# A Mamba block with its RWKV feed-forward on one core: the mix of r moved into scaled weights, the norms' small scalars moved to ScalarE, and new tables of turns

## The chip, the cores and the metric

The kernel runs on one core of a Trainium2 chip. The metric is the time on the device in microseconds (us), as the median of several runs. The core's engines work side by side, each through its own list of instructions in order, and they meet only through semaphores: TensorE (PE in the profile) multiplies matrices out of SBUF into PSUM, VectorE (DVE) and ScalarE (ACT) work elementwise on SBUF and PSUM, GpSimd (POOL) works elementwise on SBUF, and SyncE (SP) issues the transfers.

## The reference

Everything is float32: x has 4 sequences of 2048 tokens with 256 channels, the state has N = 16 columns for each channel.

```python
x = x + mamba(layernorm(x))
x = x + ffn(layernorm(x))

def mamba(x_in):
    x, z = split(x_in @ W_in)
    proj = x @ W_x                       # raw delta, B (16), C (16)
    delta = softplus(proj[..., :D] @ W_dt + b_dt)
    h_t = exp(delta_t * A) * h_{t-1} + (delta_t * x_t) * B_t      # for each of 16 columns
    y_t = sum over the columns of h_t * C_t,   y = y + x * D_param
    res = (y * silu(z)) @ W_out + x_in
    return layernorm(res) * ln_g + ln_b

def ffn(h):                              # h_prev: h of the token before, 0 at the start
    hr = mu_r * h + (1 - mu_r) * h_prev
    hk = mu_k * h + (1 - mu_k) * h_prev
    r = sigmoid(hr @ W_r.T);  k = hk @ W_k.T
    return r * (square(relu(k)) @ W_v.T)
```

## The kernel before

The 8192 tokens are cut into 16 chunks of 512 (`NT`), four to a sequence. A chunk has channels on the partitions (two halves of 128, index m, h or k) for the scan, and tokens on the partitions (four blocks of 128, `TB`) for the norms. The kernel is software-pipelined over steps t = -1 to 17. In step t the scan of chunk t runs, the part ahead of it (norm 1, the projections, softplus) is done for chunk t+1 (`pre`), the gate, the output projection and the norms 2 and 3 for chunk t-1 (`mid`), and the feed-forward for chunk t-2 (`end`). Step -1 is the head with tables of its own, steps 16 and 17 are the tail.

Each step has 16 turns, one for each state column n. In turn n:

- GpSimd makes `dbx` of column n+3 (`times_b`, 128x1024), and for the columns outside `SPLIT` the product of column n-1 with C (`times_c`). These are 16 + 9 products in a step.
- ScalarE makes the two exponentials of column n+1 into PSUM (`exps`). For three banks `da_ps` the exponential of a half must wait until VectorE is done with the half three places back. ScalarE also keeps the carries, and has all that turns, norms, activates and evacuates.
- VectorE scans column n in two halves, and does the product with C itself for the 7 columns of `SPLIT`. It also has the softplus differences, u, the gate, the affine part of norm 2, the feed-forward's mixes and its output product.
- TensorE adds the transposed product of column n - `Y_LAG` into `y_ps` (`add_up`, 8 matmuls), and does all projections and transposes in three banks `w0_ps` to `w2_ps`.

Where in a step's 16 turns each other unit stands is written out by hand, in tables: `ACT_TURN`, `VEC_TURN`, `PE_TURN` and `POOL_TURN` for the full steps, with `..._HEAD` and `..._TAIL` for both ends. `BANK` says in which of the three banks a unit's result is put. A unit waits for the unit ahead of it in its bank to be read. Since every engine goes through its list in order, a unit that has to wait holds up everything behind it, the exponentials, scans or products of the next columns among it.

What the change touches: `hT_in` on ScalarE (L596, L597) copies the transposed h out of PSUM twice, shifted by a token, once scaled by 1 - mu_k (`xk`) and once by 1 - mu_r (`xr`). `mix` on VectorE (L859) adds mu_k h and mu_r h to them, in two instructions for each half. `by_token` on TensorE (L966) multiplies `xr` with `w_rT`. The tanh of r (L681) reads the result. The norms: ScalarE sums and squares with accumulators, `rsqrt` makes `rs` (L522, L524), GpSimd makes `nm` of norm 3 (L483) and the products `nr` = `nm` x `rs` of norms 1 and 3 (`scale_mean`, L442), and ScalarE's `norm` (L501) reads them. On SyncE nothing of this stands.

## Time and profile before

| | before |
|---|---|
| median of 3 runs | 1037.73 us (1037.49 to 1039.17) |
| the profiled execution | 1038.93 us, its span 1037.2 us |
| busy: PE, DVE, ACT, POOL | 905.7, 925.7, 907.3, 939.1 us |
| mean granted TensorE clock | 0.934 of full speed |
| first and last start of GpSimd's `nm` in a step with a scan | 143.47 and 977.29 us |

The span is what the trace covers, and the profiled execution took 1.7 us more than it. All four engines are busy for 87 to 91% of the span. The share of a step is better read from a stretch of whole steps: from 203.1 to 859.1 us there are 11 of them, 59.64 us each. In the timeline each row gives start, duration, engine, line, operation and the tiles out<-in, and in brackets how long the engine was idle ahead of it and who ended that. A row of several instructions spans them all. Neighbours on one engine overlap in these rows by about 0.1 us.

### The profile page before, as it was taken

What the parts mean: (1) busy time and instruction counts of PE and PEld (TensorE: products, weight loads), DVE (VectorE), ACT (ScalarE), POOL (GpSimd) and SP (SyncE); (2) the same over time, 40 slices, a digit from 0 to 9 for tenths busy, and PEclk for the clock granted to TensorE, in tenths of its full rate; (3) what the DMA queues carried; (4) which work ended last, traced back from release to release, by engine and by line L of the source; (5) the groups of instructions that cost most, each with busy time, mean ns of one, the idle gap of its engine ahead of it and who ended that gap; (6) DMA issues with size and microseconds to landing.
All of it is one profiled execution on the core that took longest, in us unless ns stands there. A gap on an engine that the chain in (4) does not pass through costs nothing. (4 is left out here: it accounts for less than half of the span.)

```text
span 1037.2 us, 15069 instructions
## 1 busy us (share of the span) xinstructions
PE 905.7 (87%) x4728; PEld 699.3 (67%) x4728; DVE 925.7 (89%) x1003; ACT 907.3 (87%) x2041; POOL 939.1 (91%) x455
## 2 busy tenths in 40 slices
PE   6485888989898998989899898989989898996976
PEld 3254576867767686776768577676858677684954
DVE  0799899999999999999999999999999999999933
ACT  5886889999989999999989999999999999886753
POOL 0799999999999999999999999999999999999810
PEclk9797898999899998999999998999989998998998
DMA  4534454444535544463455545354554445254111
GB/s 141 218 123 185 166 203 182 163 166 179 189 135 212 187 184 158 170 223 125 183 186 183 195 150 206 129 203 161 187 219 151 178 166 207 100 206 180 62 41 41
DMA packets 51039, 172.21 MB, mean 166 GB/s; under 512 B 5392, under 2 KB 31760, under 8 KB 34576
## 3 DMA queue, kind: packets, MB, share of 16 engines
q1 hardware_dynamic: 50960, 171.25, 45.0%
q8 instruction: 38, 0.62, 0.2%
q14 instruction: 41, 0.34, 0.1%
HBM read 153.41 MB, written 9.44 MB: 157 GB/s over the span
## 5 line engine op out<-in xcount | busy, mean ns | idle before, releaser
L450 POOL TENSOR_TENSOR dbx<-u,b_ring 128x1024 f32<-128x1024 f32 x256 | 602.5, 2371 | 0.7 <-DVE u L850 0.7
L545 ACT ACTIVATE da_ps<-delta,a_neg 128x512 f32<-128x512 f32 x512 | 334.7, 682 | 38.8 <-DVE hg L802 14.1
L463 POOL TENSOR_TENSOR hg<-hg,c_ring 128x1024 f32<-128x1024 f32 x144 | 341.9, 2374 | 3.8 <-DVE hg L802 3.8
L952 PEld LDWEIGHTS y_ps<-ident,hg 128*128 128x128 f32 x2048 | 252.0, 149 | 74.0 <-issue 48.3
L952 PE MATMUL y_ps<-ident,hg 128*128 128x128 f32 x2048 | 277.1, 286 | 15.4 <-POOL hg L463 14.6
L802 DVE TENSOR_TENSOR_SCAN hg<-da_ps,carry,dbx 128x512 f32<-128x512 f32 x216 | 264.1, 1267 | 12.8 <-ACT da_ps L545 12.5
L802 DVE TENSOR_TENSOR_SCAN da_ps<-da_ps,carry,dbx 128x512 f32<-128x512 f32 x168 | 206.1, 1272 | 1.1 <-ACT da_ps L545 1.1
L809 DVE TENSOR_TENSOR hg<-da_ps,c_ring 128x1024 f32<-128x1024 f32 x112 | 137.2, 1225 | 12.0 <-DVE da_ps L802 0.5
L802 DVE TENSOR_TENSOR_SCAN hg<-da_ps,dbx 128x512 f32<-128x512 f32 x72 | 84.5, 1207 | 7.9 <-ACT da_ps L545 7.6
L972 PE MATMUL w_ps<-ident,h_tok 128*128 128x128 f32 x128 | 26.9, 350 | 60.9 <-DVE mixed L859 60.8
L959 PE MATMUL w_ps<-mixed,w_kT 128*128 128x512 f32 x128 | 64.9, 632 | 6.8 <-DVE mixed L859 3.7
L966 PE MATMUL w_ps<-w_rT,mixed 128*128 128x256 f32 x256 | 65.9, 413 | 3.2 <-DVEq L833 1.6
L802 DVE TENSOR_TENSOR_SCAN da_ps<-da_ps,dbx 128x512 f32<-128x512 f32 x56 | 65.3, 1210 | 0.1
L966 PEld LDWEIGHTS w_ps<-w_rT,mixed 128*128 128x128 f32 x256 | 52.8, 212 | 15.8 <-DVE mixed L859 3.4
L972 PEld LDWEIGHTS w_ps<-ident,h_tok 128*128 128x128 f32 x128 | 18.8, 176 | 64.7 <-DVE mixed L859 64.3
L959 PE MATMUL w_ps<-xnT,w_in 128*128 128x512 f32 x120 | 60.0, 624 | 1.6 <-ACT xnT L560 1.6
L966 PE MATMUL w_ps<-w_out,gated 128*128 128x256 f32 x256 | 60.5, 379 | 0.0
L966 PE MATMUL w_ps<-w_in,xnT 128*128 128x256 f32 x240 | 57.4, 382 | 3.0 <-ACT delta L588 3.0
L966 PE MATMUL w_ps<-w_vT,kact 128*128 128x256 f32 x256 | 58.3, 380 | 1.9 <-ACT kact L687 1.0
L959 PE MATMUL w_ps<-xT,w_dtx 128*128 128x512 f32 x124 | 58.5, 594 | 0.4 <-ACT bc_rows L657 0.4
L966 PEld LDWEIGHTS w_ps<-w_in,xnT 128*128 128x128 f32 x240 | 46.1, 193 | 17.3 <-issue 8.2
L966 PEld LDWEIGHTS w_ps<-w_vT,kact 128*128 128x128 f32 x256 | 47.3, 190 | 8.8 <-issue 1.9
(134 smaller groups left out, 1468.5 us busy)
## 6 DMA issues: line engine op xcount, KB each, us to landing
b_ring<-bc_rows_dram SPq DMA_DIRECT2D x64, 1024.0 KB, 5.3
c_ring<-bc_rows_dram SPq DMA_DIRECT2D x64, 1024.0 KB, 4.7
x_tok<-in_L_attn_x_in_dram SPq DMA_DIRECT2D x16, 512.0 KB, 5.8
res<-xn_tok SPq DMA_DIRECT2D x16, 512.0 KB, 3.2
xres<-in_L_attn_x_in_dram SPq DMA_DIRECT2D x16, 512.0 KB, 4.7
out_dram<-r_out SPq DMA_DIRECT2D x15, 512.0 KB, 3.0
bc_rows_dram<-bc_rows SPq DMA_DIRECT2D x16, 64.0 KB, 1.6
w_in<-in_L_attn_W_in_dram SPq DMA_DIRECT2D x1, 512.0 KB, 4.8
```

What stands on the lines that cost most here:

```text
L450: pool.tensor_tensor(dbx[:, n % X_RING, :, :], u[:, ip, :, :], b.to_broadcast([P, KH, LC]), ALU.mult).then_inc(s["dbx_done"], 1)
L463: pool.tensor_tensor(part, part, c_of(n).to_broadcast([P, KH, LC]), ALU.mult).then_inc(s["g_pool"], 1)
L545: act.activation(da_of(n, h), delta[:, ip, h, :], ACT.Exp, scale=a_neg[:, h, n:n + 1]).then_inc(s["da_ready"], 1)
L802: dve.tensor_tensor_scan(out, da_of(n, h), dbx[:, n % X_RING, h, :], 0.0 if first else carry[:, n, h:h + 1], ALU.mult, ALU.add).then_inc(s ...
L809: dve.tensor_tensor(hg[:, n % H_RING, :, :], da_both(n), c_of(n).to_broadcast([P, KH, LC]), ALU.mult).then_inc(s["g_vec"], 1)
L952: last = pe.matmul(y_tok[:, b, h * P:(h + 1) * P], hg[:, n % H_RING, h, b * P:(b + 1) * P], ident[:, :], is_transpose=True, start=n == 0 a ...
L959: last = pe.matmul(out, w[:, k, cols], x[:, k, :], start=k == 0, stop=k == KH - 1)
L966: last = pe.matmul(by_block(out)[:, b, :], xT_[:, k, tokens], w[:, k, :], start=b == 0 and k == 0 and not begun, stop=k == KH - 1, skip_gr ...
L972: last = pe.transpose(bank[:, j * P:(j + 1) * P], src[:, j, k * P:(k + 1) * P], ident[:, :])
```

## The change

It has four parts.

1. **r.** xr @ W_r.T is written as h @ (mu_r W_r.T) + h_prev @ ((1 - mu_r) W_r.T). ScalarE makes the two scaled copies `w_rT` and `w_r_prev` once in the head, in four instructions in place of one. In a step, `hT_in` copies h unscaled into `h_of`, VectorE's `mix` has one instruction for each half in place of two, and TensorE's `r_by_token` has 16 matmuls of 256 columns (each two instructions in the trace) in place of 8.
2. **Small scalars.** ScalarE makes `nr` of norms 1 and 3 behind `rs`, in four copies of 128x1 with a scale from a column each, and `nm` of norm 3 in one copy of 128x4. The squares of norm 3 take `nm` as bias, like those of norm 1. GpSimd has none of the three any more.
3. **Tables.** All turns and banks are new, and `Y_LAG` is 2 in place of 1.
4. The statistics of W_out are put into the carry's buffer, and `POOL_TURN` and `POOL_HEAD` are gone.

```diff
-B_LEAD, C_LAG, Y_LAG = 3, 1, 1
+B_LEAD, C_LAG, Y_LAG = 3, 1, 2
...
-POOL_TURN = dict(nm3=11, nr3=13, nr1=15)
...
+VEC_TURN = dict(mix0=3, mix1=3, gate=5, sp0=5, u0=6, sp1=9, u1=10, x20=10, x21=10, v0=12, v1=12)
...
-            def scale_mean(ln, count):
-                need(pool, ln_rs[ln], count)
-                pool.tensor_tensor(nr[ln][:, :], nm[ln][:, :], rs[ln][:, :], ALU.mult).then_inc(ln_nr[ln], 1)
...
-                    if mid and n == turn["nm3"]:
-                        need(pool, *((ln_sum_end, 2) if at_end(t) else (ln_sum[3], t)))
-                        pool.tensor_tensor(nm[3][:, :], sum3[:, :], minus_1_d[:, :], ALU.mult).then_inc(s["nm3_done"], 1)
-                    if more and n == turn["nr1"]:
-                        scale_mean(1, t + 3)
-                    if mid and n == turn["nr3"]:
-                        need(pool, s["nm3_done"], t)
-                        scale_mean(3, t)
...
+                if ln in nr:
+                    need(act, ln_rs[ln], count)
+                    for j in range(TB):
+                        last = act.activation(nr[ln][:, j:j + 1], nm[ln][:, j:j + 1], ACT.Copy, scale=rs[ln][:, j:j + 1])
+                    last.then_inc(ln_nr[ln], 1)
...
-                    act.activation(xr[:, m, 1:LC + 1], b[:, :], ACT.Copy,
-                                   scale=omr[:, m:m + 1]).then_inc(mixed_prev[m], 1)
+                    act.activation(h_of[:, m, 1:LC + 1], b[:, :], ACT.Copy).then_inc(mixed_prev[m], 1)
...
+                            if m == 0:
+                                act.wait_ge(s["omu_set"], 2)
+                                for k in range(KH):
+                                    act.activation(w_r_prev[:, k, :], turned[:, k, :], ACT.Copy, scale=omr[:, k:k + 1])
+                                    last = act.activation(w_rT[:, k, :], turned[:, k, :], ACT.Copy, scale=mur[:, k:k + 1])
...
+                        act.activation(nm[3][:, :], sum3[:, :], ACT.Copy, scale=-1.0 / D).then_inc(ln_sum[3], 1)
                     if mid and at("sq3"):
...
+                        squares(xres[:, nxt, :, :], 3, h_tok, t)
...
-                    for x, mu in ((xk, muk), (xr, mur)):
-                        part = x[:, m, 0:LC]
-                        last = dve.scalar_tensor_tensor(part, b[:, :], mu[:, m:m + 1], part, ALU.mult, ALU.add)
-                    last.then_inc(read_sem(t, f"hT{m}"), 1)
+                    part = xk[:, m, 0:LC]
+                    dve.scalar_tensor_tensor(part, b[:, :], muk[:, m:m + 1], part, ALU.mult,
+                                             ALU.add).then_inc(read_sem(t, f"hT{m}"), 1)
...
+            def r_by_token(out, v):
+
+                for b in range(2):
+                    at_b = (2 * v + b) * P
+                    for k in range(KH):
+                        pe.matmul(by_block(out)[:, b, :], h_of[:, k, at_b + 1:at_b + 1 + P], w_rT[:, k, :], start=k == 0,
+                                  stop=False)
+                    for k in range(KH):
+                        last = pe.matmul(by_block(out)[:, b, :], h_of[:, k, at_b:at_b + P], w_r_prev[:, k, :], start=False,
+                                         stop=k == KH - 1)
+                return last
```

**GpSimd, where `nm` and `nr` stood.** From a full step before (`nm` is norm 3's negative mean, `nr` a norm's bias), and then the same columns after the change:

```order
L463 TENSOR_TENSOR hg<-hg,c_ring 128x1024
L483 TENSOR_TENSOR nm<-sum,minus_d 128x4
L450 TENSOR_TENSOR dbx<-u,b_ring 128x1024 x2
```

```order
L457 TENSOR_TENSOR hg<-hg,c_ring 128x1024
L444 TENSOR_TENSOR dbx<-u,b_ring 128x1024 x3
```

The list is now products only, and nothing in it waits for ScalarE's norms.

**ScalarE, norm 3.** Before, from the evacuation of the second residual (`xres`) to the norm's output (`h_tok`); `da_ps` are the exponentials:

```order
L728 ACTIVATE xres,sum<-w_ps 128x256 x4
L545 ACTIVATE da_ps<-delta,a_neg 128x512 x2
L588 ACTIVATE delta<-w_ps 128x512
L737 ACTIVATE h_tok,sq<-xres,sum 128x256 x4
L522 ACTIVATE lv<-sq,eps 128x4
L524 ACTIVATE rs<-lv 128x4
L545 ACTIVATE da_ps<-delta,a_neg 128x512 x2
L560 ACTIVATE zs<-w_ps 128x512
L501 ACTIVATE h_tok<-xres,nr,rs 128x256 x4
```

After the change, from the same evacuation on:

```order
L723 ACTIVATE xres,sum<-w_ps 128x256 x4
L730 ACTIVATE nm<-sum 128x4
L533 ACTIVATE da_ps<-delta,a_neg 128x512 x2
L498 ACTIVATE h_tok,sq<-xres,nm 128x256 x4
L505 ACTIVATE lv<-sq,eps 128x4
L507 ACTIVATE rs<-lv 128x4
L511 ACTIVATE nr<-nm,rs 128x1 x4
L533 ACTIVATE da_ps<-delta,a_neg 128x512 x2
```

The small scalars now stand on ScalarE's own list, ahead of the next pair of exponentials. Norm 1 has the same four copies.

**TensorE, around the feed-forward's first half.** Before, from the transposes of `h_tok` to the evacuated x (`w_kT` comes some rows later):

```order
L952 MATMUL y_ps<-ident,hg 128x128 x32
L972 MATMUL w_ps<-ident,h_tok 128x128 x8
L952 MATMUL y_ps<-ident,hg 128x128 x8
L972 MATMUL w_ps<-ident,xn_tok 128x128 x8
L966 MATMUL w_ps<-w_rT,mixed 128x256 x8
L959 MATMUL w_ps<-xnT,w_in 128x512 x2
```

After the change, from the same transposes to the softplus addition (`ln_v`):

```order
L975 MATMUL w_ps<-ident,h_tok 128x128 x8
L943 MATMUL y_ps<-ident,hg 128x128 x8
L950 MATMUL w_ps<-xT,w_dtx 128x512 x2
L950 MATMUL w_ps<-mixed,w_kT 128x512 x2
L966 MATMUL w_ps<-w_rT,mixed 128x256 x2
L969 MATMUL w_ps<-w_r_prev,mixed 128x256 x2
L1079 MATMUL w_ps<-ln_v,ident 128x512
```

The pair of `w_rT` and `w_r_prev` rows stands four times there. The transposes of `xn_tok` and the projection of x now come ahead of those of `h_tok`, and the two halves of the transposed h are in two banks (0 and 2) where they shared bank 2.

## Rows read from the trace of the kernel before

**Rows 1.** GpSimd's timeline: start, duration, line, operation, tiles, [idle before]

```profile
33.73 11.65 POOL L450 TENSOR_TENSOR dbx<-u,b_ring 128x1024 f32<-128x1024 f32 x5 [0.71 <-DVE u L850]
...
143.47 0.20 POOL L483 TENSOR_TENSOR nm<-sum,minus_d 128x4 f32<-128x4 f32 x1 [0.70 <-ACTq L732]
...
561.11 0.20 POOL L483 TENSOR_TENSOR nm<-sum,minus_d 128x4 f32<-128x4 f32 x1 [1.33 <-DVE u L850]
...
918.79 0.20 POOL L483 TENSOR_TENSOR nm<-sum,minus_d 128x4 f32<-128x4 f32 x1 [0.97 <-ACTq L732]
```

**Rows 2.** Busy time by stretch: the sum of eleven steps, 203.1 to 859.1 us

```profile
sum 656.00, PE 606.02 PEld 473.04 DVE 626.80 ACT 617.84 POOL 643.34; mean PE 55.09 PEld 43.00 DVE 56.98 ACT 56.17 POOL 58.48
```

**Rows 3.** VectorE's waits, the same stretch: in total, times, longest us

```profile
DVE hg L802 <- ACT da_ps L545: 9.3, 15, 1.3
...
DVE hg L809 <- DVE da_ps L802: 0.5, 1, 0.5
```

**Rows 4.** ScalarE's waits, the same stretch

```profile
ACT xT L560 <- PE w_ps L959: 5.5, 11, 0.6
...
ACT r_out L681 <- PE w_ps L966: 3.8, 8, 0.7
...
ACT da_ps L545 <- DVE hg L809: 0.7, 3, 0.2
```

**Rows 5.** TensorE's timeline in one full step, around its longest idle stretch

```profile
500.35 1.04 PE L952 MATMUL y_ps<-ident,hg 128*128 128x128 f32 x8
501.23 3.62 PE L966 MATMUL w_ps<-w_vT,kact 128*128 128x256 f32 x16
504.68 1.89 PE L966 MATMUL w_ps<-w_in,xnT 128*128 128x256 f32 x8
...
517.53 1.12 PE L972 MATMUL w_ps<-ident,h_tok 128*128 128x128 f32 x4 [4.13 <-DVE mixed L859]
518.44 1.92 PE L952 MATMUL y_ps<-ident,hg 128*128 128x128 f32 x8
520.15 1.91 PE L972 MATMUL w_ps<-ident,xn_tok 128*128 128x128 f32 x8
521.86 4.29 PE L966 MATMUL w_ps<-w_rT,mixed 128*128 128x256 f32 x16
```

**Rows 6.** VectorE's timeline in the same step

```profile
516.74 0.74 DVE L859 SCALAR_TENSOR_TENSOR mixed<-w_ps,mur,mixed 128x512 f32<-128x512 f32 x1
517.39 2.33 DVE L802 TENSOR_TENSOR_SCAN hg<-da_ps,dbx 128x512 f32<-128x512 f32 x2
...
528.81 1.22 DVE L802 TENSOR_TENSOR_SCAN hg<-da_ps,dbx 128x512 f32<-128x512 f32 x1 [1.18 <-ACT da_ps L545]
```

**Rows 7.** ScalarE's timeline in the same step

```profile
515.18 0.67 ACT L597 ACTIVATE mixed<-w_ps,omr 128x512 f32<-128x512 f32 x1
...
540.62 0.57 ACT L564 ACTIVATE kact<-w_ps 128x512 f32<-128x512 f32 x1
...
554.30 0.30 ACT L522 ACTIVATE lv<-sq,eps 128x4 f32<-128x4 f32 x1
554.63 0.21 ACT L524 ACTIVATE rs<-lv 128x4 f32<-128x4 f32 x1
554.74 1.28 ACT L545 ACTIVATE da_ps<-delta,a_neg 128x512 f32<-128x512 f32 x2
```

**Rows 8.** All engines' timeline at the end of the last scan and in the tail

```profile
987.66 2.35 POOL L463 TENSOR_TENSOR hg<-hg,c_ring 128x1024 f32<-128x1024 f32 x1 [3.84 <-DVE hg L802]
...
1008.67 1.06 ACT L687 ACTIVATE kact<-kact 128x1024 f32<-128x1024 f32 x1
...
1014.64 1.06 PE L972 MATMUL w_ps<-ident,h_tok 128*128 128x128 f32 x8
...
1019.45 3.78 PE L959 MATMUL w_ps<-mixed,w_kT 128*128 128x512 f32 x4 [3.74 <-DVE mixed L859]
1023.02 2.81 PE L966 MATMUL w_ps<-w_rT,mixed 128*128 128x256 f32 x8
```

**Rows 9.** ScalarE's timeline in the head

```profile
9.37 2.07 ACT L501 ACTIVATE xn_tok<-x_tok,nr,rs 128x256 f32<-128x256 f32 x4 [0.32 <-POOL nr L442]
```

More of the change, by code:

```diff
@@ new lines @@
+VEC_HEAD = dict(wdtx=3, sp0=5, sp1=9, u0=9, u1=9, center=11)
+PE_HEAD = dict(xnT0=0, xnT1=0, x0=0, x1=5, bc=6, dt0=8, dt1=9, z1=9, z0=12, la0=14, la1=14, ffn=14)
+POOL_TAIL = dict(xb=13)
+ACT_TAIL = dict(prev=0, hT1=0, hT0=1, k1=3, gT0=3, gT1=3, sq20=5, sq21=5, rs2=6, k0=9, square=9, sum30=9, sum31=12,
+                sum3_set=12, sq3=12, rs3=12, silu=15, norm3=15)
+VEC_TAIL = dict(mix1=2, mix0=3, gate=3, x20=8, x21=11, v0=12, v1=14)
+PE_TAIL = dict(hT0=0, hT1=0, k1=2, gT0=2, gT1=2, wo0=3, wo1=4, k0=8, r0=9, r1=11, v0=13, v1=14)
@@ L61 @@
+TAIL_BANK = dict(hT1=1, wo1=1, k1=0, wo0=0, gT0=1, k0=2, v0=1, gT1=2, v1=2, hT0=2, r1=0, r0=2)
 W_BANKS = 3
@@ L184, in mamba_rwkv_layer @@
         mixed = sb("mixed", P, 2, KH, LC + 1)
-        xk, xr = mixed[:, 0, :, :], mixed[:, 1, :, :]
+        xk, h_of = mixed[:, 0, :, :], mixed[:, 1, :, :]
         kact = sb("kact", P, KH, LC)
         r_out = sb("r_out", P, TB, D)
+        carry_raw = carry[:, :, :].rearrange("p n k -> p (n k)")
+        w_stats = [carry_raw[:, 6 * k:6 * k + 6] for k in range(KH)]
+        w_mean = [carry_raw[:, 12 + 2 * k:14 + 2 * k] for k in range(KH)]
         W_LOADS = 13
@@ L466, in step @@
                 nxt = 1 - par
-                turn = of_step(t, POOL_HEAD, POOL_TURN, POOL_TAIL)
-                if t == -1:
-                    scale_mean(1, 1)
                 for n in range(NS):
@@ L476, in step @@
                         times_c(behind[0], behind[2])
-                    if mid and at_end(t) and n == turn["xb"]:
+                    if mid and at_end(t) and n == POOL_TAIL["xb"]:
                         need(pool, s["xres_loaded"], 16 * t)
@@ L713, in step @@
                             turned = work[m % 2][:, :].rearrange("p (k n) -> p k n", k=KH)
-                            act.activation(w[:, :, :], turned, ACT.Copy, scale=scale).then_inc(s["ffn_ev"], 1)
+                            if m == 0:
[3 more added lines that the diff above has]
+                                    last = act.activation(w_rT[:, k, :], turned[:, k, :], ACT.Copy, scale=mur[:, k:k + 1])
+                            else:
+                                last = act.activation(w[:, :, :], turned, ACT.Copy, scale=scale)
+                            last.then_inc(s["ffn_ev"], 1)
                     if pre and at("z_set"):
@@ L729, in step @@
                             last.then_inc(ln_sum_end if at_end(t) else read_sem(t, f"wo{v}"), 1)
-                    if mid and not at_end(t) and at("sum3_set"):
-                        need_all_read(act, t, ["wo0", "wo1"])
-                        act.sem_inc(ln_sum[3], 1)
-                    if mid and at("sq3"):
-                        need(act, *((ln_sum_end, 2) if at_end(t) else (ln_sum[3], t)))
-                        for j in range(TB):
-                            last = act.activation(h_tok[:, j, :], xres[:, nxt, j, :], ACT.Square, scale=-float(D),
-                                                  bias=sum3[:, j:j + 1], accum_out=sq[3][:, j:j + 1])
-                        last.then_inc(ln_sq[3], 1)
+                    if mid and at("sum3_set"):
+                        if at_end(t):
+                            need(act, ln_sum_end, 2)
+                        else:
+                            need_all_read(act, t, ["wo0", "wo1"])
+                        act.activation(nm[3][:, :], sum3[:, :], ACT.Copy, scale=-1.0 / D).then_inc(ln_sum[3], 1)
+                    if mid and at("sq3"):
+                        squares(xres[:, nxt, :, :], 3, h_tok, t)
                     if mid and at("rs3"):
-                        rsqrt(3, t, of=float(D * D))
+                        rsqrt(3, t)
                     if mid and at("norm3"):
@@ L1029, in post_unit @@
                         else:
-                            last = by_token(out, m, xr, w_rT)
+                            last = r_by_token(out, m)
                     else:
```

49 lines of the change are left out of this document (18 added, 31 removed).

## The prediction

> **What bounds the kernel now.** I read the timeline of GpSimd first, since the page gives it the largest busy share. The reader is to see where it waits. It starts its products at 33.73 us, five of them take 11.60 us to the next start (start plus duration, less the usual overlap), so one costs 2.32 us, and 25 of them 58.0 us for a step. Its `nm` starts at 143.47 and, 13 steps later, at 918.79 [rows 1]: 775.32 / 13 = 59.64 us for a step. The missing 1.64 us are its three small products (about 0.15 each) and the wait ahead of `nm`, which was 0.70 to 1.33 in the rows shown. That wait ends on ScalarE or VectorE, never the other way round. In the stretch of eleven steps nobody but TensorE waited for GpSimd, and that for 0.3 us in all. So GpSimd is the fullest engine and still follows the others; something else sets 59.64.
>
> Next the busy time by stretch and the waits. VectorE has a mean of 56.98 us busy in 59.64 [rows 2], and four kinds of waits, of which the first and last are shown, sum to 20.1 us in eleven steps, 1.83 a step [rows 3]; its work with the gaps that it cannot avoid is then 59.64 - 1.83 = 57.8. ScalarE has nine kinds of waits with a sum of 26.8, 2.44 a step [rows 4]; its need is 57.2. TensorE waits once a step for VectorE's mix, 4.13 us in the row shown, since both halves of h use one bank, and works slowly behind it [rows 5]: the granted clock there is the lower of its two levels (1.2 GHz), as the same eight transposes into `y_ps` take 1.92 us behind the idle stretch and 1.04 ahead of it. So four lists of 57.2 to 58.5 us interlock within a column or two, and 1.2 to 2.4 us of each step is scattered waiting: first for x, r, k and the rest that the late TensorE delivers [rows 4], and then VectorE for the exponential behind the silu, 1.18 us [rows 6]. The chain runs through three engines.
>
> **The change part by part.** The sum is made for a step, for the 13 between the two `nm` above, against the profiled execution of 1038.93 us (span 1037.2), which is 1.20 above the median 1037.73.
>
> VectorE sheds two mix instructions. One goes from 516.74 to 517.39 [rows 6], so 2 x 0.65 = 1.30, and its need falls to 56.5. That alone buys little, since it is no longer the longest list.
>
> GpSimd sheds its three small products and the wait. Its need is 58.0, and nothing but the products themselves can hold it.
>
> TensorE gains 8 matmuls, 16 instructions, of 256 columns. The nearest row is `w_vT`: 16 in 501.23 to 504.68, 3.45 us at full clock, and the r of before took 4.12 (521.86 to 525.98) behind the idle stretch [rows 5]. I take 3.45. It also loses the idle 4.4 us (48.6 in eleven steps), as the halves of h are in two banks, and with it the slow work. From the starts shown that is 518.44 to 520.15 in place of 0.88, 520.15 to 521.86 likewise, 0.67 of r and 0.47 of the transposes of h, 2.8 in all [rows 5]. Its need is 59.64 - 4.4 - 2.8 = 52.4 before and 55.9 after. The extra work is therefore covered, as long as no stretch of 4 us without work comes back. If that cover is gone it costs the 3.45 again, and more at the lower clock.
>
> ScalarE gains. The copy of h without a column as scale is 0.10 shorter (0.67 against 0.57 of a copy with a constant [rows 7]), twice, so -0.19 or so. `nm` adds one small copy, 0.10. Each `nr` adds a wait for its own `rs` (0.21 long, where the next instruction came after 0.11), 0.12, and four copies. The trace has no 128x1 copy with a column as scale. It is bounded by `rs`, a constant scale: 0.21 long and 0.11 to the next start, and by `lv`, which takes a column as operand: 0.30 long, so 0.20 to the next start if the extra 0.09 occupies the engine [rows 7]. I take 0.19, nearer to `lv`, since the operand is of that kind. Two groups are 2 x (0.12 + 4 x 0.19) = 1.76, at the low end 1.12. Altogether +1.67 (low end +1.03): ScalarE's need rises from 57.2 to 58.9 (58.2), which makes it the longest list.
>
> A rule of the Trainium skill speaks against the change here. ScalarE: Activation LUTs, in What ACT_TABLE_LOAD costs, says that an activation with a column operand is about 93 ns longer than with an immediate, and that neighbours overlap by 93 ns. The trace agrees on the first (0.30 against 0.21 [rows 7]); by the rule the eight copies take 8 x 0.187 = 1.5 us, by the low bound from rows 0.9.
>
> The waits then. With the new turns the silu stands in turn 6, and the exponentials' banks at that place are held by columns of `SPLIT`, on which VectorE also has its product, half of softplus and the gate; it should no longer wait there for 1.18. The feed-forward's r, k and z stand two or more turns behind what they need. One wait is built in: x is projected when both halves of `xnT` are out, takes 1.72 on TensorE, and ScalarE has about 1.3 us of exponentials in between. It was 5.5 in eleven steps, 0.5 a step, and 11 times of 11 [rows 4]. I keep 0.4 of it and let the rest go: 58.9 + 0.4 = 59.3 us a step. Thirteen steps of 59.64 - 59.3 = 0.34 give -4.4 us.
>
> The remainder. Ahead of 143.47 GpSimd is the bound, and loses 0.70 of wait and a small product: -0.9. At the end of the last scan GpSimd waits 3.84 for VectorE [rows 8], which has two mixes less in that step: -1.3 (0 if it is held by the exponentials, down to -5 if it keeps up with GpSimd). Head: `nr` came from GpSimd with 0.32 of idle time [rows 9]; ScalarE needs 0.12 + 0.76, partly under that, and the weights' four copies lie beside the first products, so +0.2. Tail: the relu and square of k, 1.06 + 0.5 [rows 8], move ahead under VectorE's affine, and `nr` and `nm` cost 1.0 in return; from the transposes of h to k (1014.64 to 1019.45) two mixes drop out, about 1.0; the last step has 16 more instructions of r ahead of v, +3.45, of which 0.3 was a wait anyway. Together -1.5 + 3.1 = +1.6.
>
> Sum: -4.4 - 0.9 - 1.3 + 0.2 + 1.6 = -4.8. 1038.93 - 4.8 = 1034.1, and less 1.20 for the median 1032.9, say **1033 us**.
>
> **The rivals.** *GpSimd's pace.* If a small copy occupies ScalarE for the low end, and some of its listed gaps were hidden waits, ScalarE's need is near 58.2 and GpSimd's 58.0 sets the step. 13 x 1.64 = 21.3, with the other terms (-0.4) gives 1038.93 - 21.7 - 1.2 = 1016; with the end of the scan at its best (-3.7 more), 1012. For it: VectorE and TensorE now have 1.5 and 2.1 us to spare. Against it: `lv` against `rs`, and that four interlocked lists never ran without 1.2 us of waits.
>
> *No change.* ScalarE keeps about 0.7 to 0.9 of its 2.44 us of waits in place of 0.4. A step is 59.6 to 59.8, and the time 1037 to 1039. The load was then only moved from one full engine to the next.
>
> *Slower: r on the chain.* In the new order TensorE does k, then all of r, then the softplus addition. From the copies of h to the tanh of r ScalarE has some 18 instructions of 0.4 to 1.3 us (seven exponentials, four sums with their readouts, the softplus of one half, a k, the table load, the silu), about 11 us by durations as in [rows 7], an estimate. TensorE needs 0.75 for the mix, 1.7 for k and 6.9 for r, with the hand-overs 9.7. The margin is 1.3. It decides when TensorE comes to k at the lower clock, as it does now: the 2.8 us lost there exceed it by 1.5, ScalarE stands at the tanh, then the exponentials behind it and the scans are late. A step is 59.3 + 1.5 = 60.8, +1.16 x 13 = +15, and the time about 1053. For it: today's r already has ScalarE waiting in 8 of 11 steps [rows 4]. Against it: the projections of x now stand just ahead of it, and keep TensorE at work.
>
> *The change does less than it says.* The waits of TensorE for the mix could stay in another place, as the halves of h now wait for x and `xnT` to be read from their banks. Such a wait is short of 4 us by the order, and I count it under the two cases above.
>
> **How the numbers follow.** Forecast, a step of 58.9 to 59.55: 1028 to 1036, 43%. GpSimd's pace or near it, 1012 to 1028: 22%. No change, 1036 to 1040: 17%. r on the chain or ScalarE keeping all its waits, 1042 to 1058: 18%. The range leaves out the best end of the second (5%) and the last from 1046 on (14%): 1015 to 1046. About 0.2%, 2 us, is what a measurement can tell from no change here. Faster by more than that, below 1035.7: 0.62; within: 0.19; slower: 0.19.
>
> **What would show each step.** GpSimd: no wait of more than 0.1 in a full step if ScalarE isn't the bound, waits for u or the scan if it is. ScalarE: busy 57.5 to 58 us a step, `nr` copies 0.28 long and 0.19 apart. VectorE: near 55.7 busy, with its waits on the exponentials grown to 2 us or more. TensorE: one `r` of 6.9 us, clock above 0.97 in full steps, no idle stretch of 4 us. The prediction is wrong if the step is below 58.5 (then ScalarE's load was overrated), or if ScalarE waits for the tanh's input.

## The result, and the profile after

| | before | after |
|---|---|---|
| median | 1038.22 us (1037.49 to 1039.17) | 1026.52 us (1025.62 to 1027.70) |
| profiled execution, span | 1038.93, 1037.2 us | 1025.62, 1023.8 us |
| start of GpSimd's first `dbx` | 33.73 | 33.38 |
| end of GpSimd's last product with C | 990.01 | 974.22 |
| from there to the span's end | 47.2 | 49.6 |

The ratio is 0.9887 with a 95% interval of 0.9870 to 0.9905: faster by 11.7 us or 1.1%, where 4.7 us were forecast. Here and below, each ratio is against the kernel before, measured beside the run. The three lower rows of the table split the difference of the spans: head -0.35, the stretch with scans -15.4 (956.3 to 940.8), tail +2.4. The ends of before are in [rows 1] and [rows 8]; those of after are these rows of GpSimd's timeline (start, duration, line, operation, tiles, [idle before]):

```profile
33.38 11.68 POOL L444 TENSOR_TENSOR dbx<-u,b_ring 128x1024 f32<-128x1024 f32 x5 [31.91 <-DVE u L842]
...
971.85 2.37 POOL L457 TENSOR_TENSOR hg<-hg,c_ring 128x1024 f32<-128x1024 f32 x1 [3.69 <-DVE hg L794]
```

A step is now read from ScalarE's `nm`, which stands once in each:

```profile
137.91 0.20 ACT L730 ACTIVATE nm<-sum 128x4 f32<-128x4 f32 x1
...
901.22 0.21 ACT L730 ACTIVATE nm<-sum 128x4 f32<-128x4 f32 x1
```

763.31 / 13 = 58.72 us for a step, against 59.64: 0.92 less, times 13 is 12.0 of the 15.4.

The busy time of eleven steps, which answers [rows 2], and beside it TensorE's mean granted clock (PEclk) from the row of one core. From 200 to 850 us before had 0.96 there.

```profile
196.75:842.90 646.15, 628.96 (x3434) 486.32 (x3433) 616.40 (x652) 625.16 (x1498) 639.90 (x276) 1.00 0.49 181
```

The columns are PE, PEld, DVE, ACT and POOL. ScalarE is busy for 56.83 us of a step (before 56.17), VectorE 56.04 (56.98), GpSimd 58.17. So GpSimd idles for 0.57 of 58.74, where it was 1.15 of 59.64. The longest waits, from 200 to 850 us (in total, times, longest), answer [rows 3] and [rows 4]:

```profile
DVE hg L794 <- ACT da_ps L533: 14.5, 25, 0.9
ACT xT L548 <- PE w_ps L950: 8.9, 11, 0.9
...
POOL hg L457 <- ACT carry L539: 5.5, 8, 1.1
...
ACT da_ps L533 <- DVE hg L794: 2.9, 11, 0.3
...
DVE da_ps L794 <- ACT da_ps L533: 2.4, 11, 0.4
```

ScalarE waited 82 times in nine kinds before, 26 times in four kinds now. Of what the late TensorE delivered, only x is left to wait for, but for 0.6 us in all. VectorE and GpSimd wait for ScalarE. The page puts the chain that ended last mostly on ScalarE:

```profile
ACT 55%; PE 25%; DVE 9%; issue 7%; DMA 2%; POOL 1%; SPq 1%; ACTq 0%; DVEq 0%; POOLq 0%
```

TensorE's stretch behind the feed-forward's first half, which answers [rows 5]:

```profile
517.70 1.95 PE L950 MATMUL w_ps<-mixed,w_kT 128*128 128x512 f32 x4 [0.38 <-DVE mixed L850]
519.49 1.02 PE L966 MATMUL w_ps<-w_rT,mixed 128*128 128x256 f32 x4
520.36 1.03 PE L969 MATMUL w_ps<-w_r_prev,mixed 128*128 128x256 f32 x4
...
525.99 1.03 PE L969 MATMUL w_ps<-w_r_prev,mixed 128*128 128x256 f32 x4
526.86 1.02 PE L1079 MATMUL w_ps<-ln_v,ident 128*128 128x512 f32 x2
```

The wait for the mix fell from 4.13 to 0.38 us, r takes 7.4 for all 32 records (519.49 to 526.86, one short wait among them), at the granted clock's higher level.

### The profile page after: what moved, and what is told of

Same layout as the page of the kernel before. It is cut to its first block, busy times and chain, and to the rows that moved or that the text cites. A ratio compares the mean times of both kernels' runs of the same rounds, so it can differ in the third digit from the quotient of the medians.

```text
span 1023.8 us, 15677 instructions
## 1 busy us (share of the span) xinstructions
PE 932.5 (91%) x4984; PEld 715.1 (70%) x4984; DVE 909.3 (89%) x970; ACT 920.2 (90%) x2188; POOL 931.9 (91%) x407
## 4 chain that ended last, share of the span: by engine, by line
ACT 55%; PE 25%; DVE 9%; issue 7%; DMA 2%; POOL 1%; SPq 1%; ACTq 0%; DVEq 0%; POOLq 0%
ACT da_ps L533 16%; PE w_ps L950 11%; PE w_ps L957 5%; DVE hg L794 4%; PE y_ps L943 3%; ACT h_tok L498 3%; DVE da_ps L794 3%; ACT xn_tok L484 3%; ACT spare L498 3%; ACT h_tok L484 2%; ACT nr L511 2%; ACT spare L490 2%; PE w_ps L1020 2%; ACT xres L723 2%; PE w_ps L975 2%
## 5 line engine op out<-in xcount | busy, mean ns | idle before, releaser
L943 PE MATMUL y_ps<-ident,hg 128*128 128x128 f32 x2048 | 251.4, 274 | 0.8 <-POOL hg L457 0.8
L943 PEld LDWEIGHTS y_ps<-ident,hg 128*128 128x128 f32 x2048 | 233.5, 142 | 24.7 <-issue 18.7
L969 PE MATMUL w_ps<-w_r_prev,mixed 128*128 128x256 f32 x256 | 65.7, 379 | 0.0
L957 PE MATMUL w_ps<-w_in,xnT 128*128 128x256 f32 x240 | 58.9, 390 | 6.2 <-ACT zs L548 6.2
L966 PEld LDWEIGHTS w_ps<-w_rT,mixed 128*128 128x128 f32 x256 | 47.7, 191 | 23.2 <-ACT kact L552 10.8
L957 PE MATMUL w_ps<-w_vT,kact 128*128 128x256 f32 x256 | 60.8, 381 | 0.5 <-ACT r_out L669 0.5
L950 PE MATMUL w_ps<-xnT,w_in 128*128 128x512 f32 x120 | 56.5, 615 | 4.3 <-ACT xnT L548 4.3
L950 PEld LDWEIGHTS w_ps<-mixed,w_kT 128*128 128x128 f32 x128 | 24.1, 199 | 49.8 <-issue 27.4
L1079 PE MATMUL w_ps<-ln_v,ident 128*128 128x512 f32 x62 | 34.9, 647 | 23.1 <-DVE w_ps L836 23.1
```

The lines of the kernel that those rows point to most:

```text
L943: last = pe.matmul(y_tok[:, b, h * P:(h + 1) * P], hg[:, n % H_RING, h, b * P:(b + 1) * P], ident[:, :], is_transpose=True, start=n == 0 a ...
L950: last = pe.matmul(out, w[:, k, cols], x[:, k, :], start=k == 0, stop=k == KH - 1)
L957: last = pe.matmul(by_block(out)[:, b, :], xT_[:, k, tokens], w[:, k, :], start=b == 0 and k == 0 and not begun, stop=k == KH - 1, skip_gr ...
L966: pe.matmul(by_block(out)[:, b, :], h_of[:, k, at_b + 1:at_b + 1 + P], w_rT[:, k, :], start=k == 0, stop=False)
L969: last = pe.matmul(by_block(out)[:, b, :], h_of[:, k, at_b:at_b + P], w_r_prev[:, k, :], start=False, stop=k == KH - 1)
```

## The experiments

### Which of the changes brings it

Three runs take the changed kernel and undo a part; the turns stay new.

`scalars_on_pool`: `nm` and `nr` are GpSimd's again.

```diff
+POOL_TURN = dict(nm3=12, nr3=13, nr1=15)
-                    for j in range(TB):
-                        last = act.activation(nr[ln][:, j:j + 1], nm[ln][:, j:j + 1], ACT.Copy, scale=rs[ln][:, j:j + 1])
```

> The changed kernel with one part undone: nm and nr are GpSimd's again (nm3 in turn 12, nr3 in 13, nr1 in 15), the folded r and all other turns stay. Theory S (ScalarE's list sets the changed kernel's step of 58.72 us: 57.5 of work, the rest waits): ScalarE loses 1.66 us a step, GpSimd gains 0.45, so the step falls to GpSimd's list and its waits, 58.4 to 58.9, and the time is 1021 to 1029. Theory G (GpSimd's pace, 58.0, plus what it waits, sets the step, and ScalarE only follows): the three products and the wait ahead of nm come on top, 59.2 to 59.7, 1032 to 1039.

Measured: 1028.25 us (1024.52 to 1029.69), ratio 0.9919 (0.9890 to 0.9947). No wait of GpSimd is left in 200 to 850 us, and it is busy for 648.99 of the 650. So the move of the scalars hardly matters here: with them GpSimd's list is full, without them the chain through ScalarE is as long.

`r_mixed_again`: r is mixed by VectorE, the scalars stay on ScalarE.

```diff
-                    part = xk[:, m, 0:LC]
+                    for x, mu in ((xk, muk), (xr, mur)):
+                        part = x[:, m, 0:LC]
```

> The changed kernel with the other part undone: r is mixed on VectorE again (two instructions for each half) and TensorE has 8 matmuls for r in place of 16; turns, banks and ScalarE's small scalars stay. Theory S: VectorE's list grows by 1.30 to 57.8, still shorter than the step, and TensorE's shrinks by 3.45; ScalarE's is 0.19 longer. Step 58.7 to 59.1, time 1026 to 1031. Rival V (what pays in the change is the shorter VectorE list): the 1.3 us come back in full, step 60.0, time 1043.

Measured: 1041.13 us, ratio 1.0042 (1.0021 to 1.0062). That is near rival V and far above theory S. The fold of r is worth 14.6 us under the new turns, 0.9 a step and more, though it takes only 1.30 us from VectorE and 0.2 from ScalarE.

`tables_only`: both are undone, by the two diffs above together.

> Only the new turns, banks and Y_LAG: both the folded r and ScalarE's small scalars are undone. If the turns carry the gain, the step is that of the longer of GpSimd's list (58.45) and VectorE's (57.8) plus waits of 0.3 to 0.8, 58.7 to 59.3, time 1026 to 1034. If the two moves of work carry it, it is the step of before, 59.6, time 1037 to 1040.

Measured: 1040.23 us, ratio 1.0032 (1.0018 to 1.0046). The new order of turns alone gains nothing; it is 2.4 us slower. Three runs then go the other way, from the old turns:

`both_moves_old_tables` is the changed kernel with the old turns and banks.

```diff
-B_LEAD, C_LAG, Y_LAG = 3, 1, 2
+B_LEAD, C_LAG, Y_LAG = 3, 1, 1
...
-VEC_TURN = dict(mix0=3, mix1=3, gate=5, sp0=5, u0=6, sp1=9, u1=10, x20=10, x21=10, v0=12, v1=12)
+VEC_TURN = dict(mix1=1, mix0=2, gate=3, sp0=8, u0=9, sp1=11, x20=11, x21=11, u1=12, v0=13, v1=13)
```

> Both moves of work with the turns, banks and Y_LAG of before. TensorE gets 3.45 us of r at the lower clock behind its idle stretch of 4 us, in the chain mix, r, x, softplus, and ScalarE 1.66 us more. If that chain sets the step before, it grows by 2 to 4 us, time 1063 to 1090. If the lists alone do (ScalarE 57.5, GpSimd 58.0), the step is 59.3 to 59.8, time 1033 to 1040.

Measured: 1103.81 us, ratio 1.0653 (1.0629 to 1.0677), more than was expected. The next two tell whose it is. `fold_old_tables` is the kernel before with the first part of the change, `scalars_old_tables` with the second:

```diff
-                            last = by_token(out, m, xr, w_rT)
+                            last = r_by_token(out, m)
```

> The kernel before with the mix of r folded into the two scaled copies of W_r alone; small scalars on GpSimd and the old turns as before. VectorE sheds 1.3 us of a step, TensorE has 3.45 more right behind its longest idle stretch, at the lower clock. If TensorE's extra work finds no cover in the old order, the r of 4.3 us becomes one of 7 to 8 and x comes that much later, ScalarE waits for it: a step of 62 to 65, the time 1070 to 1110. If it is covered, the gain of one mix less shows, 1026 to 1030, and the 66 us come from ScalarE's scalars.

Measured: 1078.91 us, ratio 1.0380 (1.0359 to 1.0401).

```diff
-POOL_TURN = dict(nm3=11, nr3=13, nr1=15)
...
+                    for j in range(TB):
+                        last = act.activation(nr[ln][:, j:j + 1], nm[ln][:, j:j + 1], ACT.Copy, scale=rs[ln][:, j:j + 1])
```

> The kernel before with the small scalars on ScalarE alone; r mixed on VectorE, the old turns. ScalarE has 1.66 us more in a step, GpSimd three small products less. If ScalarE's list is on the chain in before, a step rises by 1 to 1.7: 1050 to 1062. If it has room as r_mixed_again against tables_only says for the new turns (+0.9 us in all), the time is 1037 to 1042.

Measured: 1061.48 us, ratio 1.0217 (1.0202 to 1.0233). Under the old turns ScalarE's 1.66 us more a step cost 23 us (1.4 a step), under the new ones 0.9 in all (`r_mixed_again` against `tables_only`). Together:

| median, us | neither | scalars on ScalarE | r folded | both |
|---|---|---|---|---|
| old turns | 1038 | 1061 | 1079 | 1104 |
| new turns | 1040 | 1041 | 1028 | 1027 |

Under the old turns the two moves cost 23 and 40 us and nearly add up (66). The new turns are worth nothing by themselves, but with both moves they are worth the 77 us between the two entries of the last column. How the old order fails is seen in the waits of `fold_old_tables`:

```profile
DVE hg L811 <- ACT da_ps L547: 41.6, 12, 4.8
...
ACT r_out L683 <- PE w_ps L986: 30.6, 14, 2.8
```

and in TensorE's timeline:

```profile
655.27 1.12 PE L992 MATMUL w_ps<-ident,h_tok 128*128 128x128 f32 x4 [3.79 <-DVE mixed L867]
656.18 1.96 PE L960 MATMUL y_ps<-ident,hg 128*128 128x128 f32 x8
657.94 1.91 PE L992 MATMUL w_ps<-ident,xn_tok 128*128 128x128 f32 x8
659.65 1.77 PE L983 MATMUL w_ps<-w_rT,mixed 128*128 128x256 f32 x4
661.25 1.03 PE L986 MATMUL w_ps<-w_r_prev,mixed 128*128 128x256 f32 x4
```

The wait for the mix is still there, r begins at the clock's lower level and takes 7.7 us, ScalarE stands at the tanh for 2.8 us (30.6 in eleven steps), and VectorE behind it for the exponentials. This is the mechanism of the rival "r on the chain", in the order where it holds.

### Is VectorE's load the bound in the kernel before?

The prediction read 1.30 us less on VectorE as worth little. Three runs leave single pieces out of the kernel before. `before_one_mix_less` leaves out mu_r h, so r is not mixed right and TensorE has the same work:

```diff
-                    for x, mu in ((xk, muk), (xr, mur)):
+                    for x, mu in ((xk, muk),):
```

> The kernel before with the term mu_r h of r left out: VectorE has one mix for each half in place of two, and nothing else changes, TensorE's work included. So this is VectorE's part of the change alone, with the old turns. Theory V: the 1.3 us are on the chain and come out nearly in full until GpSimd's 58.45 and its wait bind, step 58.6 to 59.0, 1022 to 1029 us. The prediction's reading (VectorE isn't the longest list, so this alone buys little): 59.4 or more, 1034 to 1039.

Measured: 1027.73 us (1027.68 to 1028.21), ratio 0.9896 (0.9881 to 0.9911). That is 10.5 us less than the kernel before, nearly the whole gain of the change, with TensorE still idle for 3.7 us a step ahead of the transposes of h:

```profile
PE w_ps L972 <- DVE mixed L859: 40.6, 11, 3.8
```

`before_copy_less` takes 1.3 us from ScalarE instead:

```diff
-                    act.activation(xr[:, m, 1:LC + 1], b[:, :], ACT.Copy,
-                                   scale=omr[:, m:m + 1]).then_inc(mixed_prev[m], 1)
...
-                        last = dve.scalar_tensor_tensor(part, b[:, :], mu[:, m:m + 1], part, ALU.mult, ALU.add)
+                        last = dve.scalar_tensor_tensor(x[:, m, 0:LC], b[:, :], mu[:, m:m + 1], xk[:, m, 0:LC], ALU.mult, ALU.add)
```

> The kernel before without ScalarE's two copies of h scaled by 1 - mu_r (VectorE's second mix reads the other copy, so r is mixed wrongly; two mixes per half stay, TensorE as before). ScalarE sheds 1.3 us of a step, VectorE nothing. If VectorE alone is on the chain, nothing changes: 1036 to 1040. If the chain passes through both lists, as the waits of both on each other say, the gain is a half to all of what one mix less gave: 1027 to 1034. The mixes can also start 1.3 us sooner, which is part of the second case.

`before_both_less` leaves out the copy and the mix.

```diff
-                            last = by_token(out, m, xr, w_rT)
+                            last = by_token(out, m, xk, w_rT)
```

> The kernel before with r reading the mix of k (one copy and one mix per half less, so r lacks its own mix): ScalarE and VectorE both shed 1.3 us of a step. GpSimd needs 25 x 2.33 = 58.2, its three small products 0.45, and its wait ahead of nm. If these last set the step once the chain is short, it is 58.7 to 59.0, and the time that of one mix less, 1025 to 1029. If the wait ahead of nm goes as well, 58.65 or less and 1019 to 1024.

Measured: 1031.59 us, ratio 0.9931 (0.9916 to 0.9946), and 1021.40 us, ratio 0.9833 (0.9816 to 0.9849). So the mixes off VectorE give 10.5, the copies off ScalarE 6.8, both 17.0, which is their sum within the intervals. Two lists that compete for the longest would not do so; pieces that lie one behind the other on one chain do. Spread over 16 steps that is 0.66 for VectorE's 1.30, and 0.43 for ScalarE's. From the first `nm` on, 13 steps of each trace last 59.01, 59.32 and 58.77 us in place of 59.64. ScalarE's share is not that of its list alone: its two copies are 1.3 us by duration and 1.15 from start to start, and without them VectorE's mixes no longer wait for a copy (4.3 us in eleven steps before).

The waits show one way that VectorE's share takes. In `before_one_mix_less` TensorE is released sooner, and ScalarE waits less for what TensorE delivers:

```profile
ACT xT L560 <- PE w_ps L959: 2.7, 6, 0.6
...
ACT r_out L681 <- PE w_ps L966: 0.9, 2, 0.6
```

These were 5.5 and 3.8 [rows 4]. All six kinds of ScalarE's waits for TensorE fall from 20.0 to 10.5 us in eleven steps, 0.86 a step, so part of the chain may well pass through TensorE. No run separates this part.

`before_banks_apart` tests the part of the reasoning that saw the late TensorE as a cause: the halves of h in two banks, nothing else.

```diff
-            bc=2, hT1=2, z1=2, k0=0, hT0=2)
+            bc=2, hT1=0, z1=2, k0=0, hT0=2)
```

> The kernel before with one number changed: the transposed h of half 1 goes to bank 0 in place of bank 2, so TensorE no longer waits 4 us a step for the mix and no longer works at the lower clock behind it. If the late TensorE sets the step before (part of the prediction's argument), the step falls from 59.7 to 58.9 to 59.3, 1026 to 1033 us. If VectorE and ScalarE set it between them, with VectorE's mixes on the chain (theory V), it stays, 1036 to 1040.

Measured: 1039.29 us, ratio 1.0019 (1.0004 to 1.0034). TensorE's wait ahead of the transposes of h is gone, but an idle stretch of the same length stands a few instructions later, ahead of the addition into `y_ps`, for GpSimd's product, and the work behind it is slow as before:

```profile
PE y_ps L952 <- POOL hg L463: 47.2, 12, 4.3
```

```profile
518.16 1.97 PE L952 MATMUL y_ps<-ident,hg 128*128 128x128 f32 x8 [4.26 <-POOL hg L463]
```

ScalarE waits for x and k as long as before (5.5 and 3.6 us in eleven steps). So this run did not take the lateness of TensorE away, and it can't tell whether that lateness sets the step. What it shows is that two banks for h do not remove the idle 4 us by themselves. The run that has neither the long stretch nor the lower clock is `tables_only` (granted clock 1.00 from 200 to 850 us, no wait of TensorE over 1.8), and it gains nothing. But it differs in more: all four mixes stand in one turn there, and ScalarE's exponentials wait 11.7 us in eleven steps for VectorE's scans, where it was 4.3. What the late TensorE cost in the kernel before stays open.

### What bounds the kernel after

`no_prev_matmuls` leaves out the 8 matmuls of h_prev (r lacks that term).

```diff
-                    for k in range(KH):
-                        last = pe.matmul(by_block(out)[:, b, :], h_of[:, k, at_b:at_b + P], w_r_prev[:, k, :], start=False,
-                                         stop=k == KH - 1)
```

> The changed kernel with the 8 matmuls of h_prev in r left out (r lacks that term), so TensorE has 3.45 us less in a step and all else stands. If the extra work of r is covered, as the prediction said, the time stays within 3 us of the changed kernel (1024 to 1028). If TensorE's list is now on the chain (one excursion over r and wo1 stands on it), a step falls by 0.3 or more and the time to 1016 to 1022. Against both stands that TensorE, with less to do, comes to idle stretches and the lower clock before x's projection, which would cost 0.1 to 0.5 a step: 1028 to 1033.

Measured: 1026.61 us, ratio 0.9875 (0.9852 to 0.9897), as the changed kernel. The 3.45 us come back as waiting, most of it for a half of k to be read (11 times, 1.9 at most):

```profile
PE w_ps L966 <- ACT kact L552: 20.8, 11, 1.9
```

The extra work of r is covered in full.

`no_nr` leaves out the eight small copies; the norms take `nm` as bias.

```diff
-                             scalars_of(nr[1]), s["xn_done"])
+                             scalars_of(nm[1]), s["xn_done"])
```

> The changed kernel with the eight small copies of nr left out (the norms 1 and 3 take nm as bias, which is another result), so ScalarE sheds 1.5 to 1.7 us of a step and GpSimd gets nothing. If ScalarE's list is the spine that GpSimd's pace lies just beneath (products alone 25 x 2.32 = 58.0 to 58.2), a step falls from 58.7 to 58.1 to 58.3 and the time to 1018 to 1022. If ScalarE's list alone sets the step, it falls by the whole 1.6 and the time to 1003 to 1008. If VectorE, which waits for ScalarE now, carries a part of the chain of its own, the gain is under 0.3 a step and the time 1023 to 1027.

Measured: 1019.22 us, ratio 0.9822 (0.9805 to 0.9838), and in 200 to 850 us GpSimd is busy for 647.91 of 650. The gain is 7.3 us for 1.6 a step. So ScalarE's list is on the chain (VectorE's is too, by `r_mixed_again`), and GpSimd's pace of 25 products of 2.32 us stands closely beneath.

`nr_copies_twice` makes each small copy a second time, into another tile.

```diff
                     for j in range(TB):
+                        act.activation(sink[ln][:, j:j + 1], nm[ln][:, j:j + 1], ACT.Copy, scale=rs[ln][:, j:j + 1])
```

> The changed kernel with each of the eight small copies on ScalarE made twice (the second set into a buffer that nobody reads): ScalarE's list gets 8 x 0.19 = 1.5 us a step. Theory S: all of it is on the chain, step 60.2, about 15 steps, 1045 to 1050 us. Rival (ScalarE has slack and another engine binds): a third of it or less, up to 1034.

Measured: 1059.57 us, ratio 1.0201 (1.0186 to 1.0216), which is 33 us more than the changed kernel, or 2.1 for each of 16 steps from 1.5 added. The theory of one full list allowed no more than 1:1. TensorE's timeline shows where the rest is:

```profile
524.12 1.37 PE L977 MATMUL w_ps<-ident,xn_tok 128*128 128x128 f32 x8 [2.08 <-ACT xn_tok L485]
525.29 1.91 PE L945 MATMUL y_ps<-ident,hg 128*128 128x128 f32 x8
527.00 4.17 PE L952 MATMUL w_ps<-xnT,w_in 128*128 128x512 f32 x8
```

It waits longer for the late norm (2.08, where the changed kernel has 0.61) and then works at the clock's lower level: eight matmuls into `y_ps` take 1.91 in place of 1.04. x comes late, and ScalarE, which was late itself, waits once more:

```profile
529.54 0.60 ACT L550 ACTIVATE xT<-w_ps 128x512 f32<-128x512 f32 x1 [1.97 <-PE w_ps L952]
```

In the changed kernel that wait was 0.77, and TensorE's rows at the same place are these, at the clock's higher level:

```profile
508.00 1.06 PE L975 MATMUL w_ps<-ident,xn_tok 128*128 128x128 f32 x8 [0.61 <-ACT xn_tok L484]
508.90 1.04 PE L943 MATMUL y_ps<-ident,hg 128*128 128x128 f32 x8
510.19 3.67 PE L950 MATMUL w_ps<-xnT,w_in 128*128 128x512 f32 x8 [0.25 <-ACT xnT L548]
```

The same trace has the case that tells the two losses apart. In another step TensorE waits just as long, but the granted clock stays at its higher level (1.00 from 281 to 286 us, where it is 0.50 from 524.8 to 528.0), and ScalarE waits no longer for x than in the changed kernel:

```profile
280.93 1.06 PE L977 MATMUL w_ps<-ident,xn_tok 128*128 128x128 f32 x8 [2.08 <-ACT xn_tok L485]
281.83 1.04 PE L945 MATMUL y_ps<-ident,hg 128*128 128x128 f32 x8
```

```profile
285.17 0.60 ACT L550 ACTIVATE xT<-w_ps 128x512 f32<-128x512 f32 x1 [0.78 <-PE w_ps L952]
```

Of the eleven steps from 200.59 to 873.37 us, read from `nm` to `nm`, the two at the higher level throughout last 60.19 us, 1.47 more than the changed kernel's 58.72, which is the 1.5 added, 1:1. The other nine last 61.26 to 61.55, so the lower clock costs another 1.2.

`mix_apart` is `r_mixed_again` with the second half's mix a turn later.

```diff
-VEC_TURN = dict(mix0=3, mix1=3, ...
+VEC_TURN = dict(mix0=3, mix1=4, ...
```

> The kernel r_mixed_again (the new turns, r mixed on VectorE in two more instructions) with the second half's mix in turn 4 in place of 3. If what costs 1.1 us a step there is VectorE's load on the chain, wherever it stands, the time stays at 1038 to 1043. If it is that four mixes stand together ahead of one column's scans (2.6 us in a row, more than the banks of the exponentials cover), two and two cost less: 1028 to 1035.

Measured: 1054.48 us, ratio 1.0157 (1.0140 to 1.0174), outside both. Where the mix stands is no detail:

```profile
534.45 2.63 PE L945 MATMUL w_ps<-mixed,w_kT 128*128 128x512 f32 x4 [3.76 <-DVE mixed L845]
536.88 4.67 PE L952 MATMUL w_ps<-w_rT,mixed 128*128 128x256 f32 x16
```

An idle stretch of nearly 4 us is back, k takes 2.63 in place of 1.95, and ScalarE waits 19.6 us in eleven steps for k. The cover of TensorE's work hangs on a single turn.

### Can the scalars go elsewhere?

`nr_on_gpsimd` gives only `nr` to GpSimd, `nm` stays on ScalarE.

```diff
+POOL_TURN = dict(nr3=13, nr1=15)
```

> The changed kernel with nr of the norms 1 and 3 made by GpSimd in two 128x4 products (turns 13 and 15), nm of norm 3 kept on ScalarE. GpSimd's list is 58.1 + 2 x 0.15 = 58.4 plus what it waits for rs. If its pace is the next bound, a step is 58.4 to 58.6 and the time 1022 to 1027, between the version without nr and scalars_on_pool. If the wait of GpSimd for rs of norm 3 costs as it did before (0.7 to 1.3 a step for nm), a step is 58.9 or more and the time 1029 to 1035.

Measured: 1025.41 us, ratio 0.9874 (0.9859 to 0.9889). Its interval overlaps that of the changed kernel: no difference that can be told, since it fills GpSimd's list (648.93 of 650).

`nr_on_vector` gives `nr` to VectorE, as one 128x4 product of two tiles in SBUF.

```diff
+                dve.tensor_tensor(nr[ln][:, :], nm[ln][:, :], rs[ln][:, :], ALU.mult).then_inc(ln_nr[ln], 1)
```

> The changed kernel with nr of norms 1 and 3 made by VectorE in one 128x4 product each (turns 13 and 15), in place of ScalarE's eight copies; nm stays on ScalarE. If the chain that sets the step has ScalarE's list as its spine (theory S), 1.6 us a step leave it and the step falls until GpSimd's pace of 58.0 binds: 58.1 to 58.4, 1017 to 1022 us. If GpSimd's pace and its waits bind already, or if a mixed chain that leaves out turns 12 to 15 of ScalarE does, it stays at 58.6 to 58.8, 1024 to 1028.

Measured: 1037.23 us, ratio 1.0009 (0.9975 to 1.0043), with executions from 1034.91 to 1049.41. The 32 instructions of it take 31.8 us together, and two of them, of 7.40 and 5.53, 12.9 of these. Its group by line (busy us, mean ns), VectorE's timeline, and GpSimd's at the same time:

```profile
L803 DVE TENSOR_TENSOR nr<-nm,rs 128x4 f32<-128x4 f32 x32 | 31.8, 992 | 3.9 <-ACT rs L507 3.9
```

```profile
145.89 7.40 DVE L803 TENSOR_TENSOR nr<-nm,rs 128x4 f32<-128x4 f32 x1
...
159.34 0.13 DVE L803 TENSOR_TENSOR nr<-nm,rs 128x4 f32<-128x4 f32 x1
```

```profile
143.96 7.01 POOL L444 TENSOR_TENSOR dbx<-u,b_ring 128x1024 f32<-128x1024 f32 x3
150.90 2.37 POOL L457 TENSOR_TENSOR hg<-hg,c_ring 128x1024 f32<-128x1024 f32 x1
```

A product of 4 elements took 0.13 us in one place and 7.40 in another, across three whole products of GpSimd. ScalarE's norm behind the 7.40 us waited 6.08 for it. From `nm` to `nm`, the steps with the two long ones last 67.1 and 64.0 us, the other eleven 58.4 to 59.4. So VectorE is no dependable home for the scalars: 13.4 of the 14.7 us that this execution's span has over the changed kernel's lie in these two steps.

## Why the prediction was right or wrong

The sign, and the range, held. The size did not: 11.7 where 4.7 stood, and the range was wide, 31 us, with no change inside it. The term of the sum that was wrong is the 13 steps: -4.4 stood there and -12.0 was measured, a step of 58.72 where 59.3 stood. Two steps of the reasoning stand behind it, one on VectorE and one on ScalarE.

**VectorE.** The step that failed is "that alone buys little, since it is no longer the longest list". It was measured at 10.5 us in the kernel before, and the fold of r at 14.6 under the new turns. The reasoning took the period less an engine's listed waits as its need, ranked the needs, and let the longest set the step. (The text has four lists of 57.2 to 58.5 us, but these are three; TensorE's was 52.4 by its own sum.) But none of those lists was the bound; the step was a chain with pieces of VectorE and of ScalarE in it (the same text says further up that "the chain runs through three engines"), and each of them waited for the other. On such a chain a piece counts where it lies, whatever the rank of its engine: `before_one_mix_less`, `before_copy_less` and `before_both_less` show 0.66, 0.43 and their sum.

**ScalarE.** The addition was sized right. `rs` to the first copy is 0.23 us and the four copies take 0.76 to the next exponential, as forecast:

```profile
552.58 0.30 ACT L505 ACTIVATE lv<-sq,eps 128x4 f32<-128x4 f32 x1
552.91 0.20 ACT L507 ACTIVATE rs<-lv 128x4 f32<-128x4 f32 x1
553.14 0.85 ACT L511 ACTIVATE nr<-nm,rs 128x1 f32<-128x1 f32 x4
```

The sum under it was not. The need of 57.2 should have become 58.9; by the same reckoning it is now 58.72 less its waits, 12.8 / 11 = 1.16, so 57.6. Where ScalarE does not wait, its neighbours overlap by 0.1 us. With 56 waits fewer in eleven steps that gives back 0.5 of the missing 1.3. Its busy time says the same: it rose by 0.66 a step only, to 56.83, where 57.5 to 58 had been named as the sign. A second part is idle time too short to be listed: all idle time less the listed waits was 656.0 - 617.8 - 26.8 = 11.4 us in eleven steps [rows 2, 4], and is 646.15 - 625.16 - 12.8 = 8.2 now, 0.3 less a step. The remaining 0.5 is again in overlaps, at gaps too short to be listed. Ahead of the exponentials alone, ScalarE's idle time fell from 11.9 us, of which 6.8 were listed, to 2.9 (the groups of the kernel before and of the changed one, over the same eleven steps as above):

```profile
L545 ACT ACTIVATE da_ps<-delta,a_neg 128x512 f32<-128x512 f32 x352 | 229.8, 682 | 11.9 <-DVE hg L802 4.3 <-DVE carry L812 1.8 <-DVE hg L809 0.7
```

```profile
L533 ACT ACTIVATE da_ps<-delta,a_neg 128x512 f32<-128x512 f32 x352 | 228.5, 686 | 2.9 <-DVE hg L794 2.9
```

Counted over all of ScalarE's instructions in these steps, a gap of any length stood ahead of 25.5 a step before, and of 15.2 now, without the three that the new scalars bring. Ten gaps closed, five of them listed; at 0.1 us of overlap each, the other five give the 0.5.

**TensorE.** The extra 3.45 us of r are covered, as forecast (`no_prev_matmuls`), and the idle 4 us and the slow work behind them are gone. But the reason given for the latter, two banks for the halves of h, is not enough: `before_banks_apart` has them and keeps both. The need of 55.9 was too low as well, since TensorE is busy for 57.18 of a step (628.96 / 11); no run shows where the other 1.3 us lie. Whether the late TensorE was the first cause of ScalarE's scattered waits is not settled: they fell together with its lateness in `before_one_mix_less`, and nothing was gained by its loss in `tables_only`. What held was the condition: if the cover goes, the price is high, 40 us in `fold_old_tables`.

**The kept wait for x.** 0.4 a step were kept; it is 0.81 (8.9 / 11). The silu's wait of VectorE [rows 6] went as said: the scans behind the gate and the silu start without idle time. VectorE's waits for the exponentials grew from 0.85 to 1.54 us a step ((14.5 + 2.4) / 11), where 2 or more had been named as the sign.

**GpSimd's pace.** As a rival it was given 22% and 1012 to 1028, and the result lies inside it at 1026.5. Of its two conditions one came, that some of ScalarE's gaps were hidden waits; the other, a small copy at the low end of 0.11 us, did not, as the copies stand 0.19 apart. The step of 58.72 is below the 58.9 at which the forecast case began. It isn't that case in the strict sense, since GpSimd still waits for 0.57 a step; but with the small copies gone (`no_nr`) or moved (`scalars_on_pool`, `nr_on_gpsimd`) GpSimd is the bound. The prediction named 58.5 as the step below which ScalarE's load would be overrated; it was overrated already at 58.72.

**Head and tail.** Head -0.35 (forecast +0.2), tail +2.4 (forecast +1.6). What was gained ahead of the first `nm` and in the last scan is 15.4 - 12.0 = 3.4, where 2.2 stood. Here GpSimd's wait at the end did not shrink, 3.69 against 3.84: the last scan ended sooner as a whole.

**Slower: r on the chain.** It did not come; its margin held, as TensorE comes to k at the clock's higher level. The last matmul of r ends at 527.02 (525.99 + 1.03, shown above), and ScalarE reaches the tanh later than that:

```profile
527.69 1.07 ACT L669 ACTIVATE r_out<-w_ps 128x512 f32<-128x512 f32 x2
```

`fold_old_tables` shows the rival's mechanism, ScalarE standing at the tanh, with a price of 40 us. In `mix_apart` ScalarE stands at k, which comes late in the same way, with a price of 13 us.

What stays open is which single wait fixes the share of 0.66 and 0.43, and how much of the first passes through TensorE; the runs give the shares, not the links.

## What to carry to other kernels

When four engines are all busy for 87% or more and each waits a little for the others, don't rank them by their need. Take 1 us from each in turn, by leaving out work, and read the share that comes back; here two such shares added up, as pieces of one chain do. Before a run is read as a test of a cause, see in its trace that the cause is gone: in `before_banks_apart` it had only moved. A move of work and the order of turns are one change: here the moves under the old turns lost 23 to 66 us, the new turns alone gained nothing, and the new turns with r folded gave nearly all of it, since the engine that receives the work then has a covered place for it. And after a gain, look for the next bound at once: it stood 0.6 us of a step beneath, and three ways of relieving ScalarE ran into it.

## What the runs showed of the hardware

A VectorE product with both inputs in SBUF took 7.40 us for 4 columns while GpSimd ran its products back to back, and 0.13 us elsewhere (`nr_on_vector`; 30 of the 32 took 0.13 to 1.18). In these stretches VectorE's other work has an operand in PSUM and shows no such row. The Trainium skill (SBUF — State Buffer, Who interferes with whom, and its Summary: rules for kernel authors) states that VectorE with two SBUF inputs contends with a GpSimd instruction that reads SBUF, and that the later one blocks until the first is finished. The trace agrees on the blocking, but here it lasted across three of GpSimd's instructions of 2.33 us, not one.

A loss on ScalarE of 1.5 us a step cost 2.7 in nine of eleven steps and 1.5 in the other two (`nr_copies_twice`). In the nine, TensorE's granted clock went to the lower level (1.2 GHz) for 3.4 us, within 1.2 us behind a wait of 2.08 to 2.32 us and ahead of the work that ScalarE needs. In the two it stayed at the higher one (2.4 GHz), behind waits of 2.08 and 2.15 us in the same place, so the length of the wait alone does not tell which comes. In the changed kernel that wait is 0.8 us at most, and the granted clock is 1.00 in all eleven steps.
